# The rows' numbers turned by a DMA instead of TensorE, one matmul fewer for the variance, and another order on DVE and ACT

## The reference

```
ln(x, g, b)   = (x - mean) / sqrt(var + 1e-5) * g + b          (over the 512 features)
h = ln(ln(x, pw_g[pathway], pw_b[pathway]), cp_g[kind], cp_b[kind])
t = ln(x, tm_g[kind], tm_b[kind]);   s = ln(x, ms_g[scale], ms_b[scale])
m, n, r = x + (one row per batch element, from three small MLPs)
cat = [w0 h, w1 t, w2 m, w3 n, w4 r, w5 s]                     (w = softmax(aw))
x1  = x + ln(silu(cat @ int_W1 + int_b1) @ int_W2 + int_b2, int_g, int_be)
y   = clip(((x1 * style) @ weight.T) * demod + bias, -256, 256) (style, demod per batch element)
out = x1 + y
```

## Time and profile before

| | |
|---|---|
| median of 3 runs | 1159.75 us (1159.05 to 1159.75) |
| the profiled execution, and its span | 1159.39 us, 1157.6 us |
| granted PE clock over the span | 0.999 of 2.4 GHz |
| ACT, busy tenths in 40 slices | 3647475574746557375574746557375574747553 |
| PE, busy tenths in 40 slices | 5999999999999999999999999999999999999998 |

### The profile page before, as it was taken

The page is one execution under the profiler, slowest core; times in us unless marked ns, Lnnn a source line. Parts: engine busy times, 40 slices in busy tenths (PEclk is TensorE's granted clock), DMA queues, the critical chain, the costliest instruction groups (busy, mean ns, idle before and its releaser), DMA issues.

```text
span 1157.6 us, 14923 instructions
## 1 busy us (share of the span) xinstructions
PE 1137.3 (98%) x5036; PEld 925.2 (80%) x5036; DVE 933.6 (81%) x1752; ACT 676.0 (58%) x970; POOL 238.0 (21%) x268
## 2 busy tenths in 40 slices
PE   5999999999999999999999999999999999999998
PEld 4667888888888888888888888888888888888886
DVE  6898978879698787969879697896969879697836
ACT  3647475574746557375574746557375574747553
POOL 3441222213122211212212122220212212022000
PEclk9999999999999999999999999999999999999999
DMA  9953262333425233352423425333352424425001
GB/s 327 352 180 72 84 178 82 123 76 119 125 82 164 75 110 102 91 162 82 130 69 128 117 82 164 88 112 88 101 152 82 137 65 134 111 82 158 13 1 73
DMA packets 115372, 135.23 MB, mean 117 GB/s; under 512 B 69824, under 2 KB 70208, under 8 KB 115200
## 3 DMA queue, kind: packets, MB, share of 16 engines
q1 hardware_dynamic: 99872, 83.32, 25.6%
q0 software_dynamic: 14336, 50.34, 13.7%
q10 hardware_dynamic: 1088, 0.62, 0.2%
HBM read 101.74 MB, written 16.78 MB: 102 GB/s over the span
## 4 chain that ended last, share of the span: by engine, by line
PE 86%; DVE 9%; ACT 2%; issue 1%; DMA 1%; POOL 1%; SPq 0%; DVEq 0%; POOLq 0%; ACTq 0%
PE pre L1243 13%; PE pre L1247 13%; PE pre L1250 13%; PE uy L1301 5%; PE uy L1302 5%; PE uy L1304 5%; PE uy L1314 4%; PE uy L1317 4%; PE pre L1283 4%; PE uy L1315 4%; PE pre L1282 4%; PE pre L1281 4%; PE turn L1222 3%; PE pre L1264 1%; DMA ug<-x_in 1%
## 5 line engine op out<-in xcount | busy, mean ns | idle before, releaser
L435 POOL TENSOR_TENSOR ra<-vea,half 128x1 f32<-128x1 f32 x64 | 48.3, 754 | 374.9 <-DVE vea L825 374.9
L594 ACT ACTIVATE hi_a<-xT,style 128x512 fp32r<-128x512 f32 x60 | 43.5, 725 | 133.2 <-DVE xT L925 133.2
L1301 PE MATMUL uy<-hi_c,w_hi_w 128*128 128x512 f32 x256 | 101.4, 396 | 0.0
L602 ACT ACTIVATE ug<-uy,cols,dcoef 128x512 f32<-128x512 f32 x56 | 43.5, 776 | 98.5 <-PE uy L1317 98.5
L1304 PE MATMUL uy<-lo_c,w_hi_w 128*128 128x512 f32 x256 | 100.3, 392 | 0.3 <-DVE lo_c L880 0.2
L1281 PE MATMUL pre<-hi_b,w_hi_x 128*128 128x512 f32 x256 | 99.9, 390 | 0.6 <-DVE w_lo_x L1054 0.6
L1302 PE MATMUL uy<-hi_c,w_lo_w 128*128 128x512 f32 x256 | 100.0, 391 | 0.0
L1283 PE MATMUL pre<-lo_b,w_hi_x 128*128 128x512 f32 x256 | 99.7, 389 | 0.0
L1282 PE MATMUL pre<-hi_b,w_lo_x 128*128 128x512 f32 x256 | 99.6, 389 | 0.0
L857 DVE TENSOR_TENSOR lo_a<-tmp_a,hi_a 128x512 fp32r<-128x512 f32 x64 | 44.2, 690 | 66.3 <-ACT hi_a L521 66.2
L417 POOL DMA_INDIRECT gb<-pw_table,pw_ids x63 | 71.0, 1127 | 125.3 <-DMA whole_b<-gb 108.8
(11 more groups left out here) (241 smaller groups left out, 2934.1 us busy)
## 6 DMA issues: line engine op xcount, KB each, us to landing
xT<-x_turned SPq DMA_DIRECT2D x64, 256.0 KB, 2.8
out_turned<-xT SPq DMA_DIRECT2D x64, 256.0 KB, 2.0
xt<-x_in SPq DMA_DIRECT2D x62, 256.0 KB, 2.6
sel_in<-sel_ids SPq DMA_DIRECT2D x16, 192.0 KB, 2.8
raw_s<-int_w SPq DMA_DIRECT2D x2, 512.0 KB, 11.0
raw_h<-int_w SPq DMA_DIRECT2D x1, 1024.0 KB, 23.3
early_hi_w<-mlp_w SPq DMA_DIRECT2D x1, 1024.0 KB, 19.0
raw_w<-mlp_w SPq DMA_DIRECT2D x1, 1024.0 KB, 21.3
```

The lines of the kernel that those rows point to most:

```text
L1301: pe.matmul(bank, w_hi["w2"][:, c, cut], hi["c"][:, c, :], start=c == 0, stop=False)
```

## The change

From group 2 on PE doesn't turn the rows' numbers any more. expand_stat writes the four numbers of a token as 16-bit halves, first the low and then the high halves of 4 x 4 x 8 copies, 256 numbers per tile, into sq12's second half. turn_rows on SP turns the 128 x 1024 16-bit numbers by one transposing DMA into `root`. join_rows on ACT, between hidden(2) and hidden(3), puts the halves together in sq12, and pick_rows reads them there. rows_in stays for groups 0 and 1.

rows and the three tables have 128 partitions; the last 32 hold zeros, set once at the start (a memset on POOL and three copies on ACT, one of which is the copy of a table made wider).

The variance: fold_sum (DVE) adds the upper 64 partitions of the sum to the lower; high part and rest stand in the two halves of one operand, and one matmul takes both.

Orders: on ACT y_out, gate, part_halves, hidden and add_be stand in another order, and split_t, gate and u_out behind them; on DVE x_moment(f+2) and (f+3) and both expand_stats move ahead of finish, first_norm(f+2) moves behind low_rows, add_square(3) behind make_s 0, and low_h 3 into the middle of find_root; on PE the gains of t 0 to 2 stand one unit of u later; on SP load_xt(f+4) stands behind turn_tile(f+1), and turn_rows between load_xT 0 and store 2; on POOL rstd_x(f) stands behind three gathers.

```diff
@@ bank_uses
-            uses += [("rows", i + 1)] + [("gt", i + 1, c) for c in range(3)]
+            uses += [("gt", i + 1, c) for c in range(3)]
@@ build
-        rows = sb("rows", [TROWS, GROUP], F32R)
-        tab = {n: sb(f"tab_{n}", [TROWS, D], F32R) for n in "tsb"}
+        rows = sb("rows", [P, GROUP], F32R)
+        tab = {n: sb(f"tab_{n}", [P, D], F32R) for n in "tsb"}
+        numbers_apart, numbers_turned = sq12[:, 1, :].bitcast(U16), root[:].bitcast(U16)
@@ SP
+            def turn_rows(i):
+                sp.wait_ge(e_ready, (i + 1) * TPG)
+                sp.wait_ge(x1_raw, (i - 1) * C)
+                sp.dma_start_transpose(numbers_turned.rearrange("p (g k) -> p g k", k=P), numbers_apart).then_inc(rows_turned, 16)
...
                     if i:
                         store(i - 1, 1)
                         load_xT(i + 1, 0)
+                        turn_rows(i + 1)
                         store(i - 1, 2)
                         load_xT(i + 1, 1)
@@ ACT
+            def join_rows(i):
+                act.wait_ge(rows_turned, 16 * (i - 1))
+                src = numbers_turned[0:TROWS].rearrange("p (j s k) -> p j s k", j=TPG, s=2)
+                nc.scalar.activation(numbers_apart[0:TROWS].rearrange("p (j k s) -> p j s k", j=TPG, s=2), src, ACT.Copy).then_inc(rows_joined, 1)
...
                 if more:
                     y_out(i - 1, 0)
+                add_be(i, 0)
+                if more:
                     y_out(i - 1, 1)
                     gate(n * TPG)
-                add_be(i, 0)
-                if more:
                     y_out(i - 1, 2)
                     part_halves(n * TPG)
+                    y_out(i - 1, 3)
+                hidden(i, 0)
+                if more:
                     gate(n * TPG + 1)
-                    y_out(i - 1, 3)
                     part_halves(n * TPG + 1)
-                for o in range(C):
-                    hidden(i, o)
-                    if o < 3:
-                        add_be(i, o + 1)
+                hidden(i, 1)
+                add_be(i, 1)
+                hidden(i, 2)
+                if more:
+                    join_rows(n)
+                hidden(i, 3)
+                add_be(i, 2)
                 if more:
                     split_rows(n)
                 u_out(i, 0)
-                if more:
-                    split_t(n, 0)
-                    gate(n * TPG + 2)
+                add_be(i, 3)
                 u_out(i, 1)
                 if more:
+                    gate(n * TPG + 2)
+                    split_t(n, 0)
                     part_halves(n * TPG + 2)
+                u_out(i, 2)
+                if more:
                     split_t(n, 1)
-                u_out(i, 2)
@@ DVE
+            def fold_sum(i):
+                dve.wait_ge(sq_added, 3 * i + 3)
+                nc.vector.tensor_tensor(sq0[0:HALF, :], sq0[0:HALF, :], sq0[HALF:P, :], ALU.add).then_inc(sq_folded, 1)
+                dve.wait_ge(sq_folded, i + 1)
...
                 low_t(i, 2)
-                add_square(i - 1, 3)
                 make_t(i, 3)
                 make_s(i, 0)
+                add_square(i - 1, 3)
+                fold_sum(i - 1)
+                low_t(i, 3)
                 low_sum(i - 1)
-                low_t(i, 3)
+                make_s(i, 1)
                 low_s(i, 0)
-                make_s(i, 1)
...
                     finish(i - 1, 0)
                     second_norm(f)
                     first_norm(f + 1)
+                    x_moment(f + 2)
                     finish(i - 1, 1)
                     second_norm(f + 1)
-                    x_moment(f + 2)
-                    finish(i - 1, 2)
                     x_moment(f + 3)
                     expand_stat(f + 2)
-                    first_norm(f + 2)
                     expand_stat(f + 3)
+                    finish(i - 1, 2)
                     finish(i - 1, 3)
                 low_hid(i, 0)
                 low_hid(i, 1)
                 low_hid(i, 2)
+                low_hid(i, 3)
                 if more:
                     pick_rows(n)
-                low_hid(i, 3)
-                if more:
                     low_rows(n)
+                    first_norm(f + 2)
+                    make_t(n, 0)
                     second_norm(f + 2)
-                    make_t(n, 0)
                     low_t(n, 0)
@@ PE
-                pe.matmul(bank, vmat[:, 0:1].to_broadcast([P, P]), sum_r[:, 0, :], start=True, stop=False)
-                pe.matmul(bank, vmat[:, 0:1].to_broadcast([P, P]), sum_r[:, 1, :], start=False, stop=True).then_inc(turn_filled, 1)
+                pe.matmul(bank, vmat[:, 0:1].to_broadcast([P, P]), sum_r[:, 0, :], start=True, stop=True).then_inc(turn_filled, 1)
...
-                if more:
-                    rows_in(n)
                 for o in range(C):
                     unit_u(i, o)
-                    if more and o < 3:
-                        gain("t", n, o)
+                    if more and o > 0:
+                        gain("t", n, o - 1)
```

More of the change, by code:

```diff
@@ L25 @@
 TROWS = 3 * QUAD
+HALF = P // 2
 EPS = 1e-5
@@ L394, in _ @@
                         turn_tile(f + 1)
+                        if i + 2 < GROUPS:
+                            load_xt(f + 4)
                         turn_tile(f + 2)
@@ L487, in _ @@
                     gather_gc(f)
+                    rstd_x(f)
                     gather_gb(f + 2)
@@ L555, in split_rows @@
                 after(act, b_used, i)
-                nc.scalar.activation(rows[:], sel_in[:].bitcast(F32), ACT.Copy).then_inc(rows_hi, 1)
+                nc.scalar.activation(rows[0:TROWS, :], sel_in[:].bitcast(F32), ACT.Copy).then_inc(rows_hi, 1)
             def hidden(i, o):
@@ L614, in _ @@
             nc.scalar.activation(vmat[:], tmp["a"][:, 0, 0:2], ACT.Copy).then_inc(vmat_ready, 1)
+            act.wait_ge(consts_set, 2)
+            nc.scalar.activation(rows[TROWS:P, :], tab_raw["t"][TROWS:P, :], ACT.Copy)
             act.wait_ge(aw_max, 1)
@@ L624, in _ @@
             table_high("s")
+            nc.scalar.activation(tab["b"][TROWS:P, :], tab_raw["s"][TROWS:P, :], ACT.Copy)
             high("t", 2, wsm[:, 1:2])
@@ L833, in pick_rows @@
             def pick_rows(i):
-                bank = filled(dve, "rows", i)
+                if i < 2:
+                    numbers = filled(dve, "rows", i)[0:TROWS, :]
+                else:
+                    dve.wait_ge(rows_joined, i - 1)
+                    numbers = sq12[0:TROWS, 1, :]
                 dve.wait_ge(sel_loaded, 16 * (i + 1))
-                nc.vector.scalar_tensor_tensor(out=sel_in[:].bitcast(F32), in0=sel_in[:], scalar=cmp[:, 0:1], in1=bank[0:TROWS, :],
+                nc.vector.scalar_tensor_tensor(out=sel_in[:].bitcast(F32), in0=sel_in[:], scalar=cmp[:, 0:1], in1=numbers,
                                                op0=ALU.is_equal, op1=ALU.mult).then_inc(v_done, 1)
@@ new lines, in end_root, with find_root @@
+            def end_root(v, y, h):
+                link(nc.vector.scalar_tensor_tensor(out=y, in0=h, scalar=5.0, in1=y, op0=ALU.add, op1=ALU.mult))
+                link(nc.vector.tensor_tensor(h, y, y, ALU.mult))
+                link(nc.vector.scalar_tensor_tensor(out=h, in0=h, scalar=-27.0 / 1024.0, in1=v, op0=ALU.mult, op1=ALU.mult))
+                return nc.vector.scalar_tensor_tensor(out=y, in0=h, scalar=9.0 / 16.0, in1=y, op0=ALU.add, op1=ALU.mult)
+            def find_root(i, between):
@@ L913, in find_root @@
                 dve.wait_ge(var_read, i + 1)
-                inverse_root(sq[2], root[:], sq0[:], chain, root_ready)
+                begin_root(sq[2], root[:], sq0[:])
+                between()
+                end_root(sq[2], root[:], sq0[:]).then_inc(root_ready, 1)
             def make_x1(i, c):
```

76 lines of the change are left out of this document (34 added, 42 removed).

## The result

The changed kernel takes 1194.85 us (median of 4 runs, 1194.28 to 1198.55), the kernel before in the same job 1159.4 (1158.22 to 1159.75): ratio 1.031, 95% interval 1.029 to 1.034. The forecast was 1147.8 and faster. The 35 us of loss are not spread over the change: one line moved in POOL's order costs 48 us, and what is left of the change wins 13, about as forecast.

What follows compares the result with a forecast made beforehand. What TensorE has to issue, group by group, bounds the kernel. -6.2 - 3.5 - 2.1 - 0.5 + 0.3 = -12.0 us from 1159.39 gives 1147.4, median 1147.8; own range 1145 to 1151, 8 in 10 within 1144.5 to 1156.

Steps and rivals of the forecast that it cites:

- SP, POOL: Orders on these queues: load_xt(f+4) behind turn_tile(f+1), rstd_x(f) behind three gathers (about 4 us), used 18 us after x_moment(f).
- Transposes, -6.2: TensorE before u, groups 2 to 15: without four transposes of rows_in 0.44 us goes per group, 6.2 us in all.
- Variance, -3.5: TensorE's variance: one matmul instead of two, 15 x 0.235 = 3.5 us gained.
- 128 rows, -2.1 (0 to -4.3): TensorE's gains and offsets: 128 partitions instead of 96 remove slow starts; bounds 0 and 4.3 us, middle 2.1 taken.
- Group 1, -0.5: Group 1: first gain's wait for low_rows goes (-0.8), joined rows land late there (+0.3).
- The chain of the rows: Expand, transposing DMA, join, pick, split, rest, gain: no wait found; landing has 2.8 us to spare, later 2.1.
- the tight places of 0.2 to 1.0 us: lo_c 3, the bank of u and the bank of s 0: narrow margins where TensorE was forecast not to wait.
- Small waits, +0.3: Allowance of 0.3 us lost to late landings and gc waits elsewhere than group 1.
- The slower one: Joined rows come late, the join blocks ACT ahead of hidden(3), TensorE stops in 14 groups; about 1170 us; 9%.

Runs made afterwards that it cites:

- the root first: The changed kernel with one thing undone: on POOL rstd_x(f) stands ahead of the three gathers again; 1146.37 us, ratio 0.989 to the kernel before.

## Why the prediction was wrong

**The step that failed** is under SP, POOL: "rstd_x(f) is behind three gathers (about 4 us) but used 18 us after x_moment(f)." I asked when the moved instruction's own result is needed, and that answer holds: 4 us later costs nothing. I did not ask what the instructions that it was moved past would now do. The root waited for DVE, and by that wait it held three gathers until 19 us into the group; without it they leave 6 to 7 us sooner and run beside a transposition issued in the same microsecond, whose landing goes from 3.1 to 8.2 us. The trace before held the times that raise the question: the transposition issued 14.6 us into the group and used at 17.75, the gathers at 19.0, h at 24.4. What three gathers beside it would cost it did not show, since there these three never met it; the landings of 3.1 to 4.2 us that I took for this kind of DMA hold only apart from them.

**Where the 47 us are.** The profiled executions of the changed kernel and of that with the root first last 1192.5 and 1145.4 us from first to last instruction. What the starts of matmuls lie over 0.2268 us apart, added up: TensorE stands 29.9 us where h begins; h's own matmuls lose another 12.2, of which 11.1 in the 6 groups with the lower clock; u's lose 6.7, in the other eight, where they lose 1.2 with the root first. That makes 47.6 us more, and group 1 begins 0.7 us earlier in the changed kernel's execution (102.38 against 103.09).

**Transposes, -6.2:** 5.9. In the changed kernel itself x's last and u's first two start evenly.

Timeline of PE after, as the earlier trace rows.
```profile
376.18 0.39 PE L1317 MATMUL pre<-lo_b,w_hi_x 128*128 128x512 f32 x1
376.41 0.39 PE L1335 MATMUL uy<-hi_c,w_hi_w 128*128 128x512 f32 x1
376.64 0.39 PE L1336 MATMUL uy<-hi_c,w_lo_w 128*128 128x512 f32 x1
```
**Variance, -3.5:** 3.3, and there is one matmul where there were two.

**128 rows, -2.1 (0 to -4.3):** 3.6. The two nearest rows spoke each way, and I took the middle; the row of the operation itself, the gain's successor at 0.25 us, was the better guide than the variance. The rule that I weighed (the Trainium skill, "TensorE: Matmul & The Clock Gate", LDWEIGHTS: the rows of the contraction don't matter) would have given 0. The rule speaks of the load, and the load's duration agrees with it; but the start of the matmuls shifts all the same: the height alone is worth 0.23 us a group.

**Group 1, -0.5:** with the root first it takes 69.49 us instead of 70.03. But every other group became 0.93 us shorter, so what group 1 takes beyond the others went from 0.81 to 1.2 us: the term is +0.4. The wait of the first gain for low_rows is gone, as forecast; in its place the joined rows come late there, ACT waits 0.8 us for them, and u's matmuls lose 0.6 us, where I had put 0.3.

**The chain of the rows:** with the root first the transposition is issued at 496.52 and ACT joins at 501.12 without a wait, 1.5 us after the landing, where 2.1 were forecast. The expand of 256 halves takes 0.29 to 0.30 us, not 0.40. From group 2 on the tight places of 0.2 to 1.0 us all held. **Small waits, +0.3:** none to see from group 2 on. All of it, against the kernel before: -13.1 measured, -12.0 forecast. That the sum is so near is in part luck: the height gave 1.5 us more than its term, and group 1 0.9 less.

**The rivals.** The slower one, late joined rows at 9%, had the right form, a transposition that lands late and holds ACT in front of TensorE; but it was put on the new transposition, and the one that was late first is an old one that no step of my list looked at. The new one came late behind it, and only for 5.6 of the 47 us. The point from which it costs was put too high: with 1.5 us to spare instead of 2.1 it is about 1.8 us, not 2.4, and the run with turn_rows later fits that (16.3 us lost, where 2.4 would have given about 7). Its argument against, landings of 3.1 to 4.2 us, was read from a schedule in which the gathers stood elsewhere. The second rule that I weighed (the Trainium skill, "VectorE: DVE Perf Modes", Rules for kernel authors: TensorE for a 128 x 128 transposition) speaks against the change, but not here: by the runs the DMA is the better by 5.9 us once nothing collides with it, because TensorE sets the pace.

**How the two meet on the DMA queues.** The traces also record every single packet. With the root first the transposition's 1024 packets of 256 bytes start 1.17 to 2.55 us after its issue, and the last of the 4-byte packets that follow them at 2.57. With three gathers ahead the first starts at 2.80 and the last at 7.38 (medians over the groups), in between those of the gathers. A gather issued 3.1 us ahead has its last packet done at 0.97, before the first of the transposition, and costs next to nothing. One issued 0.3 us behind leaves the 1024 packets where they were, but the last 4-byte packet goes from 2.57 to 4.20, and the join with it. So packets ahead delay the transposition's start, and later ones still delay its end; it doesn't wait only for what was queued before it. **Open** is what sets the landing within 7.5 to 9.6 us, and why the granted clock fell after some stands of TensorE and not after others.

## What to carry to other kernels

An instruction that waits is also a gate for all that stands behind it in its queue. When it is moved, list what it held back, when that will now start, and what it will run beside; DMAs first, because landing times read from the old schedule don't hold in the new one. And count the slack of the old transfers too, after each microsecond that the change takes from it: the same line cost 20 us with 1.4 us more of slack and 48 without, and nothing at all with one gather instead of three. A late transfer has more than one reader, so follow it on each engine that waits for it: with two gathers h was in time, and the 4.9 us were lost some 30 us later, in u.

## What the runs showed of the hardware

- Three indirect gathers (two of 128 rows of 4 KB, one of 128 rows of 2 KB) beside a 128 x 1024 16-bit transposition raise its landing from 3.1 to 8.2 us (median), 9.6 at most; the 16 DMA engines then pass 172 to 210 GB/s, and 288 to 310 with the gathers alone.
- A matmul that contracts over 96 rows and the two or three behind it start up to 0.01 us late each, 0.02 us for the set, though its load takes the same 188 ns.
- A gather issued 0.3 us behind the same transposition leaves the starts of its 1024 packets as they were, and still the landing comes 1.5 us later; one issued 3.1 us ahead costs 0.2.
- Waits of TensorE cost more than their length: in 6 of 14 groups the granted clock was at the 1.2 GHz level after one, and h's matmuls lost 11.1 us there, beside the 29.9 us of standing. The length alone doesn't tell when: the clock fell after stands of 1.81 us (the late root on the kernel before) and 2.16, and stayed up after 2.24 and 2.76 (low_h 3 behind find_root).
